# Adding the gated product to the output in DRAM by an accumulating transfer, in an attention and feed-forward block of 16 batches

## The reference, cut to what matters

```
# block 1: a projection of the normalised x, plus a decayed scan of the normalised context,
# gathered at the patch that each row belongs to
x = x + rmsnorm(layernorm(x)) @ W_in.T + b_in + scan(rmsnorm(ctx)[..., :512])[plug]
# block 2
y      = layernorm(x)
y_prev = y shifted by one row
r  = sigmoid((mu_r * y + (1 - mu_r) * y_prev) @ W_r.T)
k  =          (mu_k * y + (1 - mu_k) * y_prev) @ W_k.T
x  = x + r * (square(relu(k)) @ W_v.T)          # the output
```

## Time and profile before

| | |
|---|---|
| median of 3 runs | 813.33 us (812.39 to 813.49) |
| profiled execution, its own time | 812.43 us |
| its span, first to last instruction | 810.8 us |
| granted TensorE clock, mean | 0.981 |
| busy: TensorE, weight loads, VectorE, ScalarE, GpSimd | 770.5, 622.9, 596.9, 401.0, 283.4 us |
| DMA, all queues | 85.81 MB, mean 106 GB/s |
| GpSimd: additions of the output (line 419), issues of the gathers (line 413) | 64 and 64 |
| stores of the output by SP (line 312) | 64 of 256 KB, 2.3 us to landing |

### The profile page before, as it was taken

The page is one execution under the profiler, slowest core; times in us unless marked ns, Lnnn a source line. Parts: engine busy times, 40 slices in busy tenths (PEclk is TensorE's granted clock), DMA queues, the critical chain, the costliest instruction groups (busy, mean ns, idle before and its releaser), DMA issues.

```text
span 810.8 us, 11013 instructions
## 1 busy us (share of the span) xinstructions
PE 770.5 (95%) x3458; PEld 622.9 (77%) x3459; DVE 596.9 (74%) x991; ACT 401.0 (49%) x649; POOL 283.4 (35%) x252
## 2 busy tenths in 40 slices
PE   3588799999999999999999999999999999999997
PEld 1467588888888888888888888888888888888875
DVE  6886987597785959778595967859596886958451
ACT  3225654455563645456364545536453654544750
POOL 8577352322415132241514224151412415142112
PEclk9699899999999999999999999999999999999999
DMA  9383226260704326070532617052351706231011
GB/s 299 121 234 65 78 67 180 55 193 12 205 32 118 129 64 182 30 203 14 122 125 68 178 39 207 0 140 107 78 169 39 207 0 152 95 73 46 2 52 53
DMA packets 44734, 85.81 MB, mean 106 GB/s; under 512 B 5104, under 2 KB 5104, under 8 KB 44688
## 3 DMA queue, kind: packets, MB, share of 16 engines
q1 hardware_dynamic: 30864, 63.02, 22.0%
q0 software_dynamic: 9216, 16.78, 13.1%
q10 hardware_dynamic: 4608, 5.51, 2.0%
HBM read 63.51 MB, written 21.79 MB: 105 GB/s over the span
## 4 chain that ended last, share of the span: by engine, by line
PE 88%; DVE 6%; POOL 2%; DMA 2%; issue 1%; POOLq 0%; DVEq 0%; ACT 0%; SPq 0%; ACTq 0%
PE bank L471 28%; PE bank L473 28%; PE bank L472 28%; PE bank L575 3%; POOL ring L413 1%; DVE scratch L944 1%; DMA gate<-in_L_xattn_W_in 1%; DVE u L902 1%; DMA ring<-s_rows,patch_now 1%; PE bank L628 0%; DVE ring L974 0%; DVE xk_lo L850 0%; DVE index_i L1105 0%; DVE bn_b L980 0%; POOL wr_lo L350 0%
## 5 line engine op out<-in xcount | busy, mean ns | idle before, releaser
L944 DVE SCALAR_TENSOR_TENSOR scratch<-turned,mus,scratch 128x512 f32<-128x512 f32 x128 | 137.9, 1088 | 48.9 <-ACT scratch L711 24.2
L419 POOL TENSOR_TENSOR gate<-gate,ring 128x512 f32<-128x512 f32 x64 | 91.1, 1575 | 193.7 <-DVE gate L999 193.7
L413 POOL DMA_INDIRECT ring<-s_rows,patch_now x64 | 107.9, 1687 | 51.3 <-DMA s_rows<-scanned 28.0
L999 DVE TENSOR_TENSOR gate<-bank,gate 128x512 f32<-128x512 f32 x64 | 43.9, 690 | 93.7 <-PE bank L473 93.6
L850 DVE TENSOR_TENSOR xr_lo<-scratch,xr_hi 128x512 fp32r<-128x512 f32 x124 | 88.1, 713 | 28.8 <-ACT xr_hi L674 28.3
L471 PE MATMUL bank<-xk_hi,wk_hi 128*128 128x512 f32 x256 | 102.4, 400 | 6.7 <-DVE xk_lo L850 6.7
L471 PE MATMUL bank<-wi_hi,xt_hi 128*128 128x512 f32 x256 | 103.6, 405 | 2.9 <-POOL xt_lo L358 2.9
L674 ACT ACTIVATE xr_hi<-scratch 128x512 fp32r<-128x512 f32 x124 | 78.3, 632 | 54.9 <-DVE scratch L944 52.7
L471 PE MATMUL bank<-wr_hi,xr_hi 128*128 128x512 f32 x256 | 101.3, 396 | 0.8 <-DVE xr_lo L850 0.8
L473 PE MATMUL bank<-xk_hi,wk_lo 128*128 128x512 f32 x256 | 101.6, 397 | 0.0
L472 PE MATMUL bank<-xk_lo,wk_hi 128*128 128x512 f32 x256 | 101.6, 397 | 0.0
(11 more groups left out here) (117 smaller groups left out, 1313.0 us busy)
## 6 DMA issues: line engine op xcount, KB each, us to landing
xt<-in_x_turned SPq DMA_DIRECT2D x16, 1024.0 KB, 5.8
ring<-in_x SPq DMA_DIRECT2D x16, 1024.0 KB, 8.0
out<-gate SPq DMA_DIRECT2D x64, 256.0 KB, 2.3
ctx_rows<-in_ctx SPq DMA_DIRECT2D x16, 512.0 KB, 8.6
s_rows<-scanned ACTq DMA_DIRECT2D x19, 256.0 KB, 2.5
gate<-in_L_xattn_W_in SPq DMA_DIRECT2D x1, 1024.0 KB, 7.7
turned<-in_L_ffn_W_r SPq DMA_DIRECT2D x1, 1024.0 KB, 17.5
ring<-s_rows,patch_now POOLq DMA_INDIRECT x64
```

What stands on the lines that cost most here:

```text
L413: pool.indirect_dma_start(ring[b.slot][:, t, :], None, s_rows[:, :], bass.IndirectOffsetOnAxis(ap=patch_now[:, t:t + 1], axis=0), compute_ ...
L419: nc.gpsimd.tensor_tensor(gate[:, t, :], gate[:, t, :], ring[b.slot][:, t, :], ALU.add).then_inc(out_ready, 1)
L944: nc.vector.scalar_tensor_tensor(scratch[:, 2 + i % 2, :], turned[:, c, 1:S + 1], mus[:, which, c:c + 1], scratch[:, i % 2, :], ALU.mult, ...
L999: nc.vector.tensor_tensor(gate[:, t, :], bank[4 + t][:, :], gate[:, t, :], ALU.mult).then_inc(gated, 1)
```

## The change

SP no longer stores the finished output tile by tile. It stores the whole of x2 of a batch, 1 MB from the ring buffer, with a plain transfer into the batch's rows of `out`, once VectorE has made it; a semaphore for each ring slot, `x2_stored`, says that it has landed. GpSimd's addition in SBUF is gone; in its place GpSimd issues a transfer that adds the gated tile to the rows in DRAM (`accum_op=ALU.add`), four per batch, the first behind a wait for that batch's `x2_stored`. `stored[t]` is now raised by that transfer. SP's load of x into a ring buffer waits for `x2_stored` of the batch that lay in it and for VectorE's last read of it (`yn_ready`) where it waited for `out_ready`, which is gone; and SP's queue waits for `x2_ready` of b where it waited for `out_ready` of each tile.

```diff
-        v_done, gated, out_ready = sems("v_done gated out_ready")
+        v_done, gated = sems("v_done gated")
+        x2_stored = [sem(f"x2_stored{i}") for i in range(RING)]
...
-                    reached(sp, out_ready, b.plus(-1), T, T)
+                    if b.plus(-1).exists(B):
+                        sp.wait_ge(x2_stored[new.slot], new.round() * 16)
+                    reached(sp, yn_ready, b.plus(-1), T, T)
                     if is_first(new, 2):
                         sp.wait_ge(w_lo_ready[WK], C)
                     load_x(new)
...
                 if b.exists(B):
-                    for t in range(T):
-                        reached(sp, out_ready, b, T, t + 1)
-                        sp.dma_start(out_rows[b.number(), :, t, :], gate[:, t, :]).then_inc(stored[t], 16)
+                    reached(sp, x2_ready, b, T, T)
+                    sp.dma_start(out_rows[b.number()], ring[b.slot][:, :, :]).then_inc(x2_stored[b.slot], 16)
 
             batches(sp, iteration, B)
+            for n in range(RING):
+                sp.wait_ge(x2_stored[n], 16 * len(range(n, B, RING)))
             for t in range(T):
                 sp.wait_ge(stored[t], 16 * B)
...
             def add_out(b, t):
+
+                if t == 0:
+                    pool.wait_ge(x2_stored[b.slot], (b.round() + 1) * 16)
                 reached(pool, gated, b, T, t + 1)
-                nc.gpsimd.tensor_tensor(gate[:, t, :], gate[:, t, :], ring[b.slot][:, t, :], ALU.add).then_inc(out_ready, 1)
+                pool.dma_start(out_rows[b.number(), :, t, :], gate[:, t, :], accum_op=ALU.add).then_inc(stored[t], 16)
```

## The result

The changed kernel takes 816.67 us (median of 6 runs, 815.17 to 817.56) against 813.39 us of the kernel before in the same session (6 runs, 812.39 to 814.68): ratio 1.0039, 95% interval 1.0025 to 1.0052. It is slower by 3.3 us, and 0.6 us above the upper end of the range given, 816.1. The profiled execution took 817.56 us, its span 816.0 us.

A forecast was written before the change was run, and what follows sets the result against it. TensorE, busy for 95% of the span, was taken to bound the kernel. Terms of -1.5 us (crossing into the last batch) and +1.1 us (tail) summed to -0.4: 812.9 us for the median, range 810.5 to 816.1.

The forecast's parts named there:

- the one on the gathers: Steady crossings: gathers queue behind two accumulations, land by 686 us, may land at 691.1; cost nothing, 1 us per us beyond.
- TensorE's idle time between 95 and 759 us: Sign of being wrong: TensorE, without idle time in the steady part before, shows some between these times.
- The deadline: Steady period: latest harmless landing of the gathers, 691.1 us, a 2.8 us margin read from TensorE's ninth matmul of the value product.
- The start-up. Nothing: Start of the kernel: SP's loads stay where they are up to 81 us, the 1 MB store follows; no cost.
- The relief of VectorE: Every batch: without GpSimd's additions VectorE gets back 3.0 us, its 3.7 us mix taking 0.75; worth nothing in the steady part.
- The crossing into the last batch: There GpSimd's four additions delay VectorE and TensorE waits 1.46 us; removing them gains 1.5 us (bounds -1.5 and 0).
- No relief: Rival, chance 0.08: GpSimd's descriptor writing holds VectorE as its additions do; crossing gives nothing, tail +1.1, 814.4 us.
- The tail: After the last product: an accumulating transfer of 4.4 us replaces addition and SP's store, 3.3 us; +1.1 (bounds -1.3 and +1.3).
- A cheap tail: Rival, chance 0.18: the last accumulation lands in 2.0 to 3.0 us, sum -1.8 to -2.8, 810.5 to 811.5 us.
- Slow accumulations: Rival, chance 0.16: accumulations hold DMA engines longer than gathers; sum +1.3 at twice, 836 us at three times, 13 crossings paying.
- the sum, -0.4: Whole kernel: -1.5 at the crossing into the last batch plus +1.1 at the tail, everything else at nothing.

The follow-up runs named there:

- run 5: Changed kernel, first crossing only: x2 store of batch 1 held until batch 2's gathers landed, batch 0's first two accumulations put behind them, loads left early; 814.70 us, 1.0019.
- run 11: Changed kernel with SP held at the first crossing until batch 2's gathers landed, and the last batch's additions made by VectorE; 811.18 us, 0.9981.
- run 10: Kernel before, with batch 14 alone finished by accumulation and the last batch's additions made by VectorE; 810.30 us, 0.9961.
- run 9: Kernel before, with only the last batch's additions made by VectorE instead of GpSimd; 811.76 us, 0.9987.
- run 8: Kernel before, with the change made for batch 14 alone (x2 stored by SP, four tiles accumulated by GpSimd); 811.89 us, 0.9991.
- run 4: Changed kernel, with batch 0's first two accumulations issued behind batch 2's gathers, SP's order unchanged; 814.45 us, 1.0018.
- run 3: Changed kernel, with only the x2 store of batch 1 held until batch 2's gathers landed, loads left early; 814.80 us, 1.0019.
- run 6: Kernel before, without accumulations, plus three 1 MB plain stores by SP to spare DRAM at the first crossing; 817.02 us, 1.0055.
- run 2: Changed kernel, with SP held at the first crossing only until the scan of batch 2 was stored; 816.14 us, 1.0046.
- run 7: Changed kernel, with the last batch finished as before: GpSimd adds, SP stores each tile, no x2 store of it; 814.96 us, 1.0025.
- run 1: Changed kernel, with SP held at the first crossing until batch 2's gathers landed, so batch 3's loads and batch 1's x2 store follow; 812.41 us, 0.9998.
- run 12: Run 11's kernel, with the x2 store moved out of every crossing, issued an iteration earlier behind the loads; 810.50 us, 0.9973 of the kernel before.

## Why the prediction was wrong

**The step that failed** is the one on the gathers: "Margin 2.8 us: the gathers may land at 691.1. Cost nothing". It took supply and deadline from one period of the steady part and let it stand for all crossings. The steady part did what it says: VectorE starts `add_x` at 692.72, 11.7 us past the turn of 681.01, and TensorE never waits. The first crossing has another supply. There the scan's store is issued 1.6 us ahead of the turn (111.67 against 113.28) instead of 4.6 (676.40 against 681.01), and the loads of x^T and x, which in the steady part go out 6 us ahead of that store (670.33 and 670.81), go out beside it. In place of "cost nothing" the gathers came 18.9 us past the turn, some 3.7 us behind the measured deadline, and cost 4.16 us. TensorE's idle time between 95 and 759 us is one of the signs of being wrong that the prediction had named. That VectorE waits 4.27 us for gathers at 126.51 stood in the trace of before; I had read the busy time of that stretch (65.8 of 65.8 us) and not what lay one wait below it.

**The deadline** itself was nearly right: 691.1 is 15.6 us past the turn of 675.48. Here is `add_x` against the turn, with the later crossings of runs 5 and 11 that lost time:

| `add_x` tile 0, us past the turn | loss, us | kernel |
|---|---|---|
| 14.39, 14.46, 14.55, 14.79 | 0, 0, 0, 0 | runs 10 and 9, before, run 8 |
| 15.43, 15.69, 16.37, 16.65 | 0.36, 0.56, 1.24, 1.48 | second and third crossing: runs 5, 11, 5, 11 |
| 16.69, 17.15, 17.89 | 1.48, 2.03, 2.67 | runs 5, 4, 3 |
| 18.83, 19.23, 19.35 | 3.72, 4.12, 4.14 | runs 6, 2, 7 |
| 18.90 | 4.16 | changed, the only one with the lower clock |
| 14.42, 14.65, 15.02 | 0, 0.36, 0.60 | runs 1, 11, 12: 0.7 to 0.9 us more behind `add_x`, with the wait for the load of x |

In every row of the second to the fourth line the first number less the second is 15.1 to 15.2. So the deadline lies there, each us behind it costs 1 us, as the prediction had it, and the lower clock adds about 0.4 us (18.90 less 15.15 is 3.75, measured 4.16). The prediction had put it 0.4 to 0.5 us too late. It took the ninth matmul, at 665.45. The code waits for each low part ahead of the first of its three matmuls, which is the seventh, 0.46 us earlier:

```profile
664.99 0.40 PE L471 MATMUL bank<-wv_hi,xr_hi 128*128 128x512 f32 x1
```

The kernel before had some 0.6 us to spare at the first crossing, and 2.3 us in the period that the prediction read (`add_x` at 688.33).

**"The start-up. Nothing"** looked at the loads up to 81 us and at the store behind them, and stopped one iteration early. The loads of the next iteration, at 111.22, are the ones that moved by 15 us, from 126.39.

**What held.** The relief of VectorE: the mix of 3.7 us is gone, and 128 mixes take 797 ns each. The crossing into the last batch: forecast -1.5, measured -1.45 and, in run 8, -1.5; "No relief" is out, since GpSimd's issues don't hold VectorE. The tail: forecast +1.1, measured +1.17; the accumulation's 4.4 us were 4.2, and GpSimd issued it 0.2 us later behind VectorE's product than its addition had started, so the closeness of the two sums is in part luck. "A cheap tail" did not come: the estimate of 2.6 us from the Trainium skill, DMA: Bandwidth & Descriptors, section Anatomy of one DMA, is 1.6 us under the measured landing. "Slow accumulations" is out as a mechanism, since the queue's share doubled and no more (13.1% to 25.9%); it had named the right symptom, VectorE's wait in front of `add_x` tile 0, but as a price in each of 13 crossings for a slow transfer, not as one crossing for 3.5 MB set free. Its sign was right for another reason. What the sum, -0.4, lacks is one term of +4.2.

## What to carry to other kernels

A queue that waits in order is often an unwritten schedule: removing the wait moves every transfer behind it, and each place where they now start must be checked for what they meet there, the first periods of a pipeline above all. Where a steady period has slack, look in the trace of before for the crossing in which the same wait is longest; that one has the least, and it decides. And if an engine's help is worth something only in one batch, change that batch alone: run 10 has the crossing's gain, with that of VectorE's tail on top (0.996), and a sixteenth of the accumulating traffic.

## What the runs showed of the hardware that I had not expected

The lower clock does not follow from an idle time of 2 us alone. Behind 2.08 us in the changed kernel's profile the granted clock stood at 0.50 for some 3 us. Behind 2.00, 2.12 and 2.14 us at the same place in runs 6, 2 and 7 it stood at 1.00 in every slice of 5 us up to 160 us. Nor did it cost much: the other three waited 1.0 us a second time where the changed kernel at the lower clock waited 0.19 us, and its loss is only some 0.4 us above theirs for the same lateness.

The scan's store of 256 KB, 2.0 us to landing in the kernel before, took 3.8 us behind two accumulations alone (run 1), 6.0 us beside 3 MB of plain stores (run 6) and 7.5 us with the two accumulations and 3.5 MB, though the 3.5 MB came from another queue and mostly behind it; the DMA engines were at a share of 1.05 and 407 GB/s there:

```profile
116.00:118.00 2.00, 2.00 (x10) 1.64 (x9) 1.23 (x2) 1.64 (x3) 0.00 (x0) 1.00 1.05 407
```

In the profile of before the program ends with GpSimd, not with the last landing. The closing instructions of before (line 97; duration ns, then start) show GpSimd's lasting until 810.6, 0.6 us past SP's, which had waited for the last store:

```profile
L97 POOLq DRAIN  x1: 4176/4176/4176, 806.4 to 806.4; - x1
...
L97 SPq DRAIN  x1: 7/7/7, 810.0 to 810.0; - x1
```

In run 10, where GpSimd has nothing to do in the last batch, its closing step starts at 771.6 and is no longer last, and the end came 0.2 us behind SP's. It is not so in every execution: in run 7's profile, with the same last addition by GpSimd, its closing step lasts 2.7 us and ends at 811.7, and SP's comes last, at 812.9. How much of run 10's 1.2 us at the tail is this and how much the shorter addition was not separated.
